# Attention bodies: projections one place forward, three banks in turn, and x1 made by ScalarE and GpSimd

## The reference

```python
x = x + tanh(g_xattn[0]) * mha(layernorm(x), ctx_1024, ctx_1024, Wq, bq, Wk, bk, Wv, bv, Wo, bo)   # 16 heads of 32
x = x + tanh(g_ffn[0]) * ffn(layernorm(x), clip_x, clip_down, w_gate, w_up, w_down)                # 1408 inner columns
# mha: softmax(q k^T / sqrt(32)) v, then Wo and bo
# ffn: fake-quantized input and weights, silu(gate) * up, fake-quantized again, then w_down
# fake-quantization: clip(round(x / s), -128, 127) * s; for activations s comes from the maximum over the whole tensor
```

## Time and profile before

| | |
|---|---|
| median of 3 runs | 1706.5 us (1705.53 to 1708.16) |
| the profiled execution | 1703.26 us, span 1701.3 us |
| busy share of the span | TensorE 94%, VectorE 77%, ScalarE 49%, GpSimd 33% |
| mean granted TensorE clock | 0.986 of full speed |
| chain that ended last | TensorE 61%, VectorE 15%, ScalarE 9%, issue 6%, DMA 4% |

### The profile page before, as it was taken

How to read it: one execution, slowest core, us unless ns; L and a number is a source line. 1 busy time by engine, 2 the same in 40 slices (tenths; PEclk the granted TensorE clock), 3 DMA queues, 4 the chain that set the end, 5 groups by cost and what they waited for, 6 DMA issues and landing times.

```text
span 1701.3 us, 31195 instructions
## 1 busy us (share of the span) xinstructions
PE 1597.2 (94%) x11750; PEld 751.3 (44%) x11750; DVE 1307.3 (77%) x2087; ACT 840.7 (49%) x1122; POOL 554.9 (33%) x782
## 2 busy tenths in 40 slices
PE   4899999999999999999999999987999999989988
PEld 2354444444445444444444444434444444434433
DVE  5658788688787887878878787677687778778876
ACT  4453543625436344353453534424677777758341
POOL 4432523425234242351433514122000000006878
PEclk9999999999999999999999999999899999999999
DMA  8697878778797688985978769535344443026998
GB/s 244 151 231 174 178 181 183 174 181 187 183 190 182 166 187 180 193 178 159 205 179 187 192 157 182 151 92 201 118 186 185 185 185 143 26 74 243 417 423 310
DMA packets 301108, 320.75 MB, mean 189 GB/s; under 512 B 176432, under 2 KB 225584, under 8 KB 298032
## 3 DMA queue, kind: packets, MB, share of 16 engines
q1 hardware_dynamic: 299248, 318.72, 69.0%
q10 hardware_dynamic: 1728, 0.27, 0.1%
HBM read 180.49 MB, written 100.27 MB: 165 GB/s over the span
## 4 chain that ended last, share of the span: by engine, by line
PE 61%; DVE 15%; ACT 9%; issue 6%; DMA 4%; SPq 2%; POOL 2%; DVEq 0%; ACTq 0%; POOLq 0%
PE spair L1624 11%; PE bank L1399 10%; PE bank L1511 10%; PE bank L1401 9%; PE bank L1400 9%; PE spair L1488 5%; DVE mx L1044 4%; PE bank L1652 3%; ACT pr L767 2%; PE spair L1463 2%; ACT ffn_work L880 2%; DMA out_dram<-yh 1%; DVE bst L994 1%; ACT wf L837 1%; POOL yh L725 1%
## 5 line engine op out<-in xcount | busy, mean ns | idle before, releaser
L1044 DVE TENSOR_REDUCE mx<-spair 128x4 f32<-128x1024 f32 x256 | 301.1, 1217 | 35.3 <-PE spair L1463 34.7
L767 ACT ACTIVATE pr<-spair 128x1024 f32<-128x1024 f32 x256 | 258.0, 1019 | 113.4 <-PE spair L1488 113.4
L1021 DVE SCALAR_TENSOR_TENSOR parts<-bank,bqk,parts 128x512 f16<-128x512 f32 x128 | 96.0, 750 | 163.8 <-ACT parts L756 162.4
L1624 PE MATMUL spair<-ffn_work,wgT 128*128 128x512 bf16 x704 | 182.5, 382 | 1.0 <-ACT ffn_work L922 1.0
L1624 PE MATMUL spair<-ffn_work,wuT 128*128 128x512 bf16 x704 | 181.8, 381 | 0.0
L1488 PE MATMUL spair<-stacks 128*128 128x256 f16 x1024 | 152.7, 276 | 14.6 <-ACT pr L767 10.5
L756 ACT ACTIVATE parts<-bank,bqk 128x512 f16<-128x512 f32 x128 | 87.7, 686 | 155.9 <-PE bank L1401 155.9
L880 ACT ACTIVATE ffn_work<-spair,gsc 128x512 f32<-128x512 f32 x176 | 118.2, 680 | 78.7 <-PE spair L1624 78.7
L630 POOL TENSOR_TENSOR cl<-cbuf,ch 128x512 f16<-128x512 f32 x64 | 77.0, 1205 | 227.0 <-ACT ch L744 227.0
L1511 PE MATMUL bank<-pr,v 128*32 128x256 f32 x2048 | 137.9, 387 | 13.7 <-ACT pr L767 8.6
L1293 DVE SCALAR_TENSOR_TENSOR hb<-spair,gsc,ffn_work 128x512 f32<-128x512 f32 x132 | 98.8, 748 | 54.8 <-ACT ffn_work L880 36.1
(11 more groups left out here) (193 smaller groups left out, 3368.3 us busy)
## 6 DMA issues: line engine op xcount, KB each, us to landing
stacks<-qk_spill SPq DMA_DIRECT2D x384, 128.0 KB, 3.9
qk_spill<-parts SPq DMA_DIRECT2D x64, 512.0 KB, 5.6
h_spill<-hb SPq DMA_DIRECT2D x10, 2816.0 KB, 9.2
x<-out_dram SPq DMA_DIRECT2D x27, 1024.0 KB, 11.1
xbuf<-in_x_dram SPq DMA_DIRECT2D x16, 1024.0 KB, 7.1
cbuf<-in_ctx_dram SPq DMA_DIRECT2D x16, 1024.0 KB, 6.7
xres<-in_x_dram SPq DMA_DIRECT2D x16, 1024.0 KB, 5.6
out_dram<-xres SPq DMA_DIRECT2D x16, 1024.0 KB, 4.5
```

The source lines that it names most:

```text
L767: act.activation(pr[:, u % 4, :, :, :].rearrange("p a b q -> p (a b q)"), spair[u % 2][:, :, :].rearrange("p a q -> p (a q)"), ACT.Exp, sc ...
L1021: dve.scalar_tensor_tensor(out=parts[:, c, 2 * w + 1, :], in0=pj[(g + 1) % 3][:, :], scalar=bqk[:, w, c:c + 1], in1=parts[:, c, 2 * w, :], ...
L1044: dve.tensor_reduce(mx[:, h:h + 2, b, :], spair[u % 2][:, :, :].rearrange("p a (q k) -> p a q k", q=KH), AX_X, ALU.max).then_inc(max_done, 1)
L1624: last = pe.matmul(spair[k % 2][:, s, :], w[:, t, kc * P:kc * P + P], xqT[:, par, kc, :], start=(kc == 0), stop=(kc == KC - 1))
```

## The change

```diff
+        def turn_bank(i, k):
+            if i == 0:
+                return pj[(k + 1) % 3 if k < 8 else k % 3]
+            return pj[(i + k) % 3]
         def x1_bank(j, t):
-            return pj[t % 2] if j == LAST else pj[t % 3]
+            return pj[t % 2] if j == LAST else turn_bank(j + 1, 12 + t)
# GpSimd
+            def x1_add(j, t):
+                wait(pool, x1_scaled, j * NT + t + 1)
+                wait(pool, res_bias, j * NT + t + 1)
+                pool.tensor_tensor(xres[:, t, :], xres[:, t, :], ndev[:, t, :], ALU.add).then_inc(x1_ready, 1)
                 o_low(j, NGR - 1)
+                if j < LAST:
+                    for t in range(NT):
+                        x1_add(j, t)
                 x1_rstds(j)
# ScalarE
+            def x1_scale(j, t):
+                wait(act, o_mm, j * NT + t + 1)
+                wait(act, x1_max, j)
+                act.activation(ndev[:, t, :], x1_bank(j, t)[:, :], ACT.Identity,
+                               scale=small[:, TGX256:TGX256 + 1]).then_inc(x1_scaled, 1)
                     for t in range(1, NT):
                         v_copy(i, t)
+                    for t in range(NT):
+                        x1_scale(j, t)
# VectorE
-                    if i == LAST:
-                        x1_tile(j, 0)
-                        for u in range(10, 16):
-                            key_max(i, u)
-                        for t in range(1, NT):
-                            x1_tile(j, t)
-                    else:
-                        for t in range(NT):
-                            x1_tile(j, t)
-                            if t < 3:
-                                key_max(i, 10 + 2 * t)
-                                key_max(i, 11 + 2 * t)
+                    for u in range(10, 16):
+                        key_max(i, u)
# TensorE
             def vproj(i, t, par):
                 if t < 3:
-                    wait(pe, qk_lo, i * 8 + (8, 6, 7)[t])
+                    wait(pe, qk_lo, i * 8 + ((8, 6, 7) if i == 0 else (6, 7, 8))[t])
...
+                if i is not None:
+                    qk(i, 2, par, before)
                 for g in range(NGR - 1):
                     score(j, 2 * g + 2)
                     pv(j, g)
                     score(j, 2 * g + 3)
-                    if i is not None and g + 2 < 8:
-                        qk(i, g + 2, par, before)
+                    if i is not None:
+                        if g + 3 < 8:
+                            qk(i, g + 3, par, before)
+                        else:
+                            vproj(i, g - 5, par)
                 if i is not None:
-                    vproj(i, 0, par)
                     max_pair(i, 0)
                 pv(j, NGR - 1)
                 if i is not None:
-                    for t in range(1, NT):
+                    for t in range(2, NT):
                         vproj(i, t, par)
-                        max_pair(i, t)
+                        max_pair(i, t - 1)
                 for t in range(NT) if i is not None else range(1, NT):
                     oproj(j, t, i)
                     if i is not None:
-                        max_pair(i, NT + t)
+                        max_pair(i, NT - 1 + t)
+                if i is not None:
+                    max_pair(i, 7)
```

More of the change, by code:

```diff
@@ L221, in gated_block_kernel @@
         x1_far = sem("x1_far")
+        x1_scaled = sem("x1_scaled")
         warm = sem("warm")
@@ L755, in qk_high @@
                 wait(act, spilled[c], i * 16)
-                act.activation(parts[:, c, 2 * w, :], pj[(g + 1) % 3][:, :], ACT.Identity,
+                act.activation(parts[:, c, 2 * w, :], turn_bank(i, g)[:, :], ACT.Identity,
                                bias=bqk[:, w, c:c + 1]).then_inc(qk_hi, 1)
@@ L760, in v_copy @@
                 wait(act, v_mm, i * NT + t + 1)
-                act.activation(v[:, t, :], pj[(2 + t) % 3][:, :], ACT.Copy, scale=1.0 / WS).then_inc(v_ready, 1)
+                act.activation(v[:, t, :], turn_bank(i, 8 + t)[:, :], ACT.Copy, scale=1.0 / WS).then_inc(v_ready, 1)
             def exps(j, u):
@@ L1020, in qk_low @@
                 wait(dve, qk_hi, i * 8 + g + 1)
-                dve.scalar_tensor_tensor(out=parts[:, c, 2 * w + 1, :], in0=pj[(g + 1) % 3][:, :], scalar=bqk[:, w, c:c + 1],
+                dve.scalar_tensor_tensor(out=parts[:, c, 2 * w + 1, :], in0=turn_bank(i, g)[:, :], scalar=bqk[:, w, c:c + 1],
                                          in1=parts[:, c, 2 * w, :], op0=ALU.add, op1=ALU.subtract).then_inc(qk_lo, 1)
@@ L1419, in qk @@
                     wait(pe, v_ready, i * NT)
-                three(pj[(g + 1) % 3][:, :],
+                three(turn_bank(i, g)[:, :],
                       [([wT[w][:, k, s, c * P:c * P + P] for s in range(2)], [src[:, k, s, :] for s in range(2)])
@@ L1425, in vproj @@
                 if t < 3:
-                    wait(pe, qk_lo, i * 8 + (8, 6, 7)[t])
+                    wait(pe, qk_lo, i * 8 + ((8, 6, 7) if i == 0 else (6, 7, 8))[t])
                 else:
                     wait(pe, v_ready, i * NT + 1)
-                three(pj[(2 + t) % 3][:, :],
+                three(turn_bank(i, 8 + t)[:, :],
                       [([cT[:, par, k, s, t * P:t * P + P] for s in range(2)], [wT[2][:, k, s, :] for s in range(2)])
```

## The result

The changed kernel takes 1725.4 us (median of 4 runs, 1724.7 to 1726.3) against 1706.0 before: a ratio of 1.0112, 95% interval 1.0094 to 1.0129, so it is slower by 19.4 us (by the interval 16 to 22), beyond the 0.2% named in the prediction. Forecast were 1729 us, within 1712 to 1737. In a later series of runs the ratio was 1.0128 (1.011 to 1.0146).

The account below looks back on a forecast made before the run. TensorE, busy nearly everywhere, was taken as the bound. +9.5 us without the clock and +12.8 for clock falls make +22.3: 1703.26 becomes 1725.6, plus 3.2 for the median 1728.8, say 1729 us; range 1712 to 1737.

Parts of the forecast that it names:

- The head: score0 to pv0, with qk2 between score1 and score2: 4.02 us in place of 2.64, grows by 1.38 a body.
- The tail: Pair 6 to pair 7 without a projection: bare 2.84 us, 2.45 idle, in place of 3.03; shorter by 0.19 a body.
- pv3 and pair 2: pv3's 0.44 us wait for norm goes in 14 bodies (-6.2); pair 2's shrinks by a third, 0.15, in 15 (-2.2).
- x1: x1 moved from VectorE to ScalarE and GpSimd: nothing waits for what is freed or for the adds; worth 0.
- The sum without the clock: All bodies, head, tail and removed waits: 17.9 - 6.2 - 2.2 = +9.5 us, between +5 and +18.
- The clock: Behind the new hole ahead of pair 7: TensorE's clock falls in 8 of 15 bodies, 1.6 us each, +12.8 us.
- Rivals D and E: D: pair 7's wait is short, 1678 us, chance 0.04; E: waits cancel, within 3.4 us of 1706.5, chance 0.06.
- Rival B: Same bare wait at pair 7, but the clock holds: +9.5, about 1716 us; chance 0.22.
- Rival C: Clock falls nearly every time, or pv3 keeps its wait as well: about 1740 us; chance 0.13.

Follow-up runs that it names:

- split_qk2: Kernel before with qk2 cut in two, six matmuls between score1 and score2, six in the old place: 1686.7 us, ratio 0.9896.
- tail_only: Kernel before with no projection between the last two max pairs (it goes ahead of pair 6), head unchanged: 1751.8 us, ratio 1.0279.
- x1_only: Kernel before with only x1 made by ScalarE and GpSimd, TensorE's order unchanged: 1705.9 us, ratio 1.0001.
- order_only: Changed kernel with x1 still made by VectorE's x1_tile, so TensorE's new order alone: 1728.9 us, ratio 1.0134.
- hole_half: Changed kernel with six of twelve matmuls of the next qk0 computed once more between pairs 6 and 7, 14 of 15 bodies: 1713.2 us, ratio 1.005.
- hole_filled: Changed kernel with qk0 of the next group computed twice, first between pairs 6 and 7, in 14 of 15 bodies: 1717.6 us, ratio 1.0072.

## Why the prediction was right

*The head.* Said: 4.02 us from score0 to pv0. Measured: 4.01. The two waits for exponentials in it are gone, and split_qk2 shows their worth separately, 18.7 us in 15 bodies.

*The tail.* Said: pair 7 takes the bare 2.84 us, idle 2.45. Measured: 2.84 and 2.45, in every body. tail_only shows it alone at about 36 us besides falls. The row for it came from one place in the trace of before where the same pair was followed by nothing.

*pv3 and pair 2.* Said: 0.44 gone, and 0.15 of the other. Measured: score8 to pv3 0.53 us (611.59 to 612.12), with norm(2) done 1.4 us ahead of pv3 (said some 0.9), and pair 2's excess over a regular step of 3.03 fell by 0.18, from 0.44. The third that the prediction took had no row behind it; it came near. In the three bodies with the longer weight pieces pair 1's wait shrank by 0.17 instead.

*x1.* Said: worth 0 on three engines. Measured: x1_only 1.0001; an add took 1.27 us in place of the mean of 1.33 taken, `x1_scale` 0.69 in place of 0.6, without effect. The last add of a body began at 582.57 and qk2 at 592.70, some 10 us later. Maxima beside adds took 2.35 and 2.36 us. The one thing I had not seen is that VectorE's `x1_tile` would have been late with this order (2.5 us of idle engine in order_only); so x1 on three engines is worth 0 in the old order and some 3 us of gain in the new one.

*The sum without the clock.* Said: +1.19 - 0.44 - 0.15 = +0.60 us a body, +9.5 in all. Measured: 70.38 - 69.83 = +0.55 a body, +8.1 us in hole_half.

*The clock.* Said: falls behind the new hole in about half the bodies, at 1.6 us each, +12.8. Measured: ten and eight falls in 14 bodies, 1.3 to 1.7 us each, and 11 us between the changed kernel and hole_half. hole_filled and hole_half settle the cause: the falls went away with the idle time, although the filler computes nothing of use. The share of a half rested on two falls behind four holes, and that is thin: the counts in profiles with this wait are seven, eight, ten and ten, so that the term came so near is in part luck. The reason given for 1.6 in place of 1.65 holds: in seven of the ten bodies the fall began up to 0.54 us before the hole's end (297.8 against pair 7 at 298.31), and there it cost least. The Trainium skill's advice on idle gaps between bursts (TensorE: Matmul & The Clock Gate, Why this matters for your kernels), by which holes of this length are harmless, does not hold in this kernel: holes of 2.45 us brought ten and eight falls in 14. Here the measurement decides.

Forecast and result differ by 3.6 us. The sum of 22.3 stands against 19.4 measured, 2.9 of it: 1.4 in the part without the clock (9.5 against 8.1), 1.5 in the clock (12.8 against the 11.3 that are left). The rest is the median of before, 1706.5 in the forecast and 1706.0 in the result, and the rounding to 1729. Rivals D and E fell with the 2.84 us from pair 6 to pair 7. Rival B has its number in hole_half, 8.1 above before: it is what the change would have cost had the clock held. Rival C's fifteen falls did not come up.

What stays open: why a given one of these equal holes brings a fall and another does not. The profiles show only that it changes from one execution to the next. Between 1.05 us, which brought none, and 2.45 us no length was tried in these bodies.

## What to carry to other kernels

Before you move a unit of work to cover a wait, look at what it covered where it stood; the price of that place is often visible once in the same trace, at an edge of the loop where nothing follows. Cover is divisible: 1.2 us of wait needs half a projection, and taking a half from a slot with slack gained 18.7 us where taking a whole one from a slot without slack lost 19.4. A hole of 2.45 us in TensorE was dearer than its length here, since the clock fell at it in more than half of the cases; useless matmuls in it were a good test for that, and half a filling was enough. And when an engine beside the bound is nearly full, its work can't be moved freely either: both of my moves of a 2.3 us instruction of VectorE only sent the wait elsewhere.

## What the runs showed of the hardware that I had not expected

- Equal holes of 2.45 us of idle TensorE went with the low clock in ten of 14 bodies in one execution and eight in another, not the same ones; with 1.05 us left of the hole it fell in none of 14. A fall lasted 3.4 us and began anywhere from 0.5 us before the hole's end to 1.2 us behind it in the changed kernel's profiles, up to 1.5 us behind it in tail_only.
- The falls may give a little back (not shown by itself): where the clock held, score0 waited for a DMA in seven bodies (hole_filled) and five (hole_half), in the two profiles of the changed kernel in one and three.
- The start, up to the first `turn_max`, lay between 80.0 and 83.9 us; in the seven that came at 82.4 us or later the granted clock had fallen at 45 to 47 us, in the seven others not. It limits what a comparison of two single profiles can tell here.
